# Group 1's values by seven products instead of eight, with M's sums on VectorE and new orders on ScalarE, VectorE and TensorE

## The chip, the cores and the metric

The kernel runs on one core of a Trainium2 chip. The metric is the device time of one execution in microseconds; several executions give a median. The profile is of one execution.

## The reference, cut to what matters

The input is 64 graphs of 128 nodes with 512 features each, an adjacency of 128x128 for each graph, and three 512x512 matrices.

```
h = maximum(layernorm(x), 0.0)
output = einsum('bni,io->bno', h, weight)            # the values
alpha = einsum('bno,bmo->bnm', h @ wq, h @ wk)
alpha = maximum(alpha, 0.0) * (adj != 0)
alpha = softmax(alpha, axis=1)
x = x + einsum('bnm,bmo->bno', alpha, output)
```

## The kernel before, in words

**Groups.** The 64 graphs are worked in 16 groups of 4, groups 0 to 15. The kernel first folds wq and wk into one matrix M, so that the scores are h M h'. Each group then has two large products, h with M (called t in the names) and h with the weight (called v), then the scores (s_bank, 48 matmuls of 128 columns), the softmax, and the output, the product of probabilities and values (12 matmuls of 512 columns). Every operand is split into a float16 high half and a float16 low half, and every product is three matmuls: high by high, high by low, low by high.

**Eight and seven products.** The plain form of a large product (`whole_product_v`, `whole_product_t`) is 48 matmuls of 512 columns. From group 2 on (`FIRST = 2`) both are made by a Strassen-like scheme (`product_v`, `product_t`): seven products P1 to P7 of 12 matmuls each, of 256 columns, into the PSUM banks TA, TB, TE (t) and VA, VB, VE (v). It needs four sums of quadrants of h (S1 to S4, `sums_of_h`, made on GpSimd, split by `hi_of_sum` on ScalarE and `lows_of_sums` on GpSimd, and transposed by DMA), four sums of the weight (wt) and of M (mt), a copy of P1 and of P5 by ScalarE (`copy_p1_t`, `copy_p5_t` and the same for v), and two additions on VectorE (`sum_x`, `sum_c22`). Groups 0 and 1 use the plain form.

**Order.** All orders are written out by hand, one in-order queue for each engine, with semaphores between them. Before group g's period, its h must be ready: VectorE takes the statistics (`stats`, L831, and the aggregate L834), GpSimd makes scale and shift (`layernorm_scales`, five small operations, L405 to L412), ScalarE normalises (`normalise_h`, L537, four graphs) and makes the high halves (`hi_of_h`, L547), GpSimd makes the low halves (L417) and S1 (L425), S3 (L428), S2 (L432), S4 (L436), where S1 waits for all four normalised graphs. SyncE's queue then issues the DMA transposes.

Two places in ScalarE's order matter. The high halves of S1 and S3 of group 3 (L552) stand ahead of `copy_p1_t` of group 2 (L574), and those of S2 and S4 of group 3 ahead of `hi_of_p` of group 1 (L656), the high halves of the probabilities. TensorE's P2 of t in group 2 waits for `copy_p1_t`, since P2 adds into the bank that the copy reads. TensorE's output products of group 1 (`outs`, L1175 to L1177) wait for the low halves of the probabilities (L908, VectorE), which wait for L656.

Of the kernel before, what the change touches and what calls it, by code (L numbers as in the profile page):

```python
# [5 lines left out]
def graph_attention_kernel(nc, x, adj, weight, wq, wk, out):  # L6
# [24 lines left out]
    FIRST = 2  # L31
    LOOPED = FIRST + 1
# [30 lines left out]
    def made_v(g, n):  # L63

        if isinstance(g, int) and g == LAST and n in (N_P2, N_P6):
            n = N_P2 + N_P6 - n
        return made(g, n)
# [4 lines left out]

    def sums(g, n):

        return 4 * g + (n - 4 * FIRST)

# [9 lines left out]
    with ctx:  # L86
# [44 lines left out]
        mt32 = spare  # L131
# [42 lines left out]
        M_BANK = [bank[k][:] for k in range(K)]  # L174

        def v_bank(g):

            return M_BANK if g == 1 else [bank[VB][:], bank[VE][:], bank[FREE][:], bank[TA][:]]


        def out_bank(g):

            if isinstance(g, int) and g == 0:
                return [bank[VB][:], bank[VE][:], bank[FREE][:], s_flat]
# [85 lines left out]
        def sum_turn(i, j):  # L270

            return i * (UNROLL // 2) + j // 2

# [3 lines left out]
        def _(sp):  # L277
# [98 lines left out]
        def _(pool):  # L376
# [106 lines left out]
            nc.gpsimd.tensor_tensor(mt32[:, T3], m32[:, HK:, HD:], m32[:, 0:HK, HD:], ALU.subtract).then_inc(mt_summed, 1)  # L483
            pool.wait_ge(mt_summed, 1)
            nc.gpsimd.tensor_tensor(mt32[:, T2], m32[:, HK:, HD:], mt32[:, T1], ALU.subtract).then_inc(mt_summed, 1)
            layernorm_scales(2)
            pool.wait_ge(mt_summed, 3)
            nc.gpsimd.tensor_tensor(mt32[:, T4], m32[:, HK:, :HD], mt32[:, T2], ALU.subtract).then_inc(mt_summed, 1)
            lo_of_h(2, 0, 0)
            lo_of_h(2, 0, 1)  # L490
            sum_s1(2)
            sum_s3(2)
            lo_of_h(2, 0, 2)
            lo_of_h(2, 0, 3)
            sum_s2(2)
            sum_s4(2)
# [24 lines left out]
            o = x_sb[:, LAST % UNROLL, 0]  # L521
# [3 lines left out]
        def _(act):  # L525
# [14 lines left out]
            def hi_of_h(g, s, b, turns=0, sum_turns=0):  # L540
# [4 lines left out]
                if b == 0 and not (isinstance(sum_turns, int) and sum_turns == 0):  # L545
                    act.wait_ge(sT_landed[s], 2 * 16 * sum_turns)
# [20 lines left out]
            def copy_p1_t(g):  # L567
# [45 lines left out]
            def hi_of_v22(g):  # L613
                act.wait_ge(v_summed, done(g, 2))
# [20 lines left out]
            def hi_of_whole_v(g, b):  # L635
# [4 lines left out]
                nc.scalar.activation(v_hi[:, b], v_bank(g)[b], ACT.Copy, scale=T_SCALE).then_inc(v_hi_made, 1)  # L640
# [780 lines left out]
```

## Time and profile before

| | us |
|---|---|
| median of 3 runs | 414.24 (414.03 to 414.66) |
| profiled execution, its own time | 414.27 |
| its span in the trace | 412.4 |
| busy: PE / DVE / ACT / POOL | 405.8 / 298.1 / 277.8 / 264.5 |

PE is TensorE, DVE is VectorE, ACT is ScalarE, POOL is GpSimd. The time outside the span is 1.9 us. TensorE's granted clock is 1.00 in every slice, which is the 2.4 GHz level. A busy time close to the span means that the engine is hardly ever without work; for the others, the idle time is spent waiting, and costs something only where TensorE waits for them.

### The profile page before, as it was taken

How to read it: one execution, taken by the hardware profiler on the slowest of the kernel's cores; microseconds unless marked ns; L12 is line 12 of the kernel's file. 1: busy time of each engine (PE TensorE's matmuls, PEld its weight loads, DVE VectorE, ACT ScalarE, POOL GpSimd, SP SyncE). 2: the span in 40 equal slices, each digit the busy share in tenths (PEclk: the TensorE clock that was granted, in tenths of full speed). 3: DMA queues.
4: the chain of work that ended last, by engine and by line, in shares of the span. 5: the costliest groups of instructions: out<-in, count | busy, mean ns of one | idle time of the engine just before them, and what ended most of it. 6: DMA issues, size and time to landing. Idle time of an engine off the chain costs nothing.

```text
span 412.4 us, 9484 instructions
## 1 busy us (share of the span) xinstructions
PE 405.8 (98%) x3581; PEld 321.9 (78%) x3581; DVE 298.1 (72%) x569; ACT 277.8 (67%) x590; POOL 264.5 (64%) x284
## 2 busy tenths in 40 slices
PE   8999999999999999999999999999999999999995
PEld 5444545979798897979798797979889797979883
DVE  5797789895867776776767777676777667556565
ACT  4749887766867677766777776776867776643534
POOL 0767896979495876859495775939577584910003
PEclk9999999999999999999999999999999999999999
DMA  8973858998969897896979497896988599393022
GB/s 299 367 98 69 215 105 224 225 206 209 218 170 191 237 155 210 193 206 183 188 219 192 131 240 200 200 214 174 188 252 157 154 219 234 41 187 100 2 103 102
DMA packets 161641, 75.03 MB, mean 182 GB/s; under 512 B 135360, under 2 KB 143808, under 8 KB 161600
## 3 DMA queue, kind: packets, MB, share of 16 engines
q1 hardware_dynamic: 161024, 73.55, 77.4%
q10 hardware_dynamic: 576, 0.92, 0.6%
q8 instruction: 28, 0.46, 0.5%
q14 instruction: 13, 0.11, 0.1%
HBM read 24.12 MB, written 16.78 MB: 99 GB/s over the span
## 4 chain that ended last, share of the span: by engine, by line
PE 82%; DVE 7%; ACT 4%; POOL 3%; issue 2%; DMA 2%; SPq 1%; DVEq 0%; ACTq 0%; POOLq 0%
PE bank L1139 10%; PE bank L1142 10%; PE bank L1141 10%; PE bank L1154 9%; PE bank L1157 9%; PE bank L1156 9%; PE s_bank L1170 3%; PE s_bank L1169 3%; PE s_bank L1168 3%; PE bank L1175 2%; PE bank L1177 2%; PE bank L1176 2%; DMA x_sb<-in_x 2%; POOL hn_lo L417 1%; ACT h L537 1%
## 5 line engine op out<-in xcount | busy, mean ns | idle before, releaser
L417 POOL TENSOR_TENSOR hn_lo<-h,hn_hi 128x512 f16<-128x512 f32 x64 | 74.5, 1174 | 54.0 <-ACT hn_hi L547 53.7
L537 ACT ACTIVATE h<-x_sb,shift,rstd 128x512 f32<-128x512 f32 x64 | 49.9, 804 | 23.6 <-POOL shift L412 23.3
L443 POOL TENSOR_TENSOR hn_lo<-s,hn_hi 128x512 f16<-128x512 f32 x56 | 63.3, 1161 | 0.3 <-ACT hn_hi L552 0.3
L1156 PE MATMUL bank<-wt_lo,hT_hi 128*128 128x256 f16 x224 | 61.1, 273 | 0.0
L1141 PE MATMUL bank<-hT_lo,mt_hi 128*128 128x256 f16 x224 | 61.1, 273 | 0.0
L1154 PE MATMUL bank<-wt_hi,hT_hi 128*128 128x256 f16 x224 | 61.1, 273 | 0.0
L1142 PE MATMUL bank<-hT_hi,mt_lo 128*128 128x256 f16 x224 | 61.1, 273 | 0.0
L1139 PE MATMUL bank<-hT_hi,mt_hi 128*128 128x256 f16 x224 | 61.1, 273 | 0.0
L1157 PE MATMUL bank<-wt_hi,hT_lo 128*128 128x256 f16 x224 | 61.1, 273 | 0.0
L552 ACT ACTIVATE hn_hi<-s 128x512 f16<-128x512 f32 x56 | 33.7, 625 | 24.1 <-POOL s L432 19.7
L1157 PE MATMUL bank<-w_hi,hT_lo 128*128 128x256 f16 x168 | 45.8, 273 | 0.0
L1156 PE MATMUL bank<-w_lo,hT_hi 128*128 128x256 f16 x168 | 45.8, 273 | 0.0
L1139 PE MATMUL bank<-hT_hi,m_hi 128*128 128x256 f16 x168 | 45.8, 273 | 0.0
L1142 PE MATMUL bank<-hT_hi,m_lo 128*128 128x256 f16 x168 | 45.8, 273 | 0.0
L1141 PE MATMUL bank<-hT_lo,m_hi 128*128 128x256 f16 x168 | 45.8, 273 | 0.0
L1154 PE MATMUL bank<-w_hi,hT_hi 128*128 128x256 f16 x168 | 45.8, 273 | 0.0
L845 DVE SCALAR_TENSOR_TENSOR tT_lo<-bank,tT_hi 128x512 f16<-128x512 f32 x42 | 28.9, 689 | 22.7 <-ACT tT_hi L605 17.2
L850 DVE SCALAR_TENSOR_TENSOR v_lo<-bank,v_hi 128x512 f16<-128x512 f32 x42 | 28.7, 684 | 21.6 <-ACT v_hi L623 21.6
L1168 PE MATMUL s_bank<-tT_hi,hT_hi 128*128 128x128 f16 x256 | 43.7, 219 | 0.0
L1169 PE MATMUL s_bank<-tT_lo,hT_hi 128*128 128x128 f16 x256 | 43.7, 219 | 0.0
L1170 PE MATMUL s_bank<-tT_hi,hT_lo 128*128 128x128 f16 x256 | 43.7, 219 | 0.0
L547 ACT ACTIVATE hn_hi<-h 128x512 f16<-128x512 f32 x64 | 39.2, 618 | 0.1
(166 smaller groups left out, 1105.0 us busy)
## 6 DMA issues: line engine op xcount, KB each, us to landing
out_h<-x_sb SPq DMA_DIRECT2D x62, 256.0 KB, 2.1
x_sb<-in_x SPq DMA_DIRECT2D x15, 1024.0 KB, 5.5
adj_sb<-in_adj SPq DMA_DIRECT2D x16, 256.0 KB, 5.3
hn_hi<-in_L_gnn_wq SPq DMA_DIRECT2D x4, 256.0 KB, 5.6
x_sb<-in_x SPq DMA_DIRECT2D x2, 512.0 KB, 7.2
w_sb<-in_L_gnn_weight SPq DMA_DIRECT2D x2, 512.0 KB, 8.6
hn_lo<-in_L_gnn_wk SPq DMA_DIRECT2D x2, 256.0 KB, 3.6
hn_lo<-in_L_gnn_wk ACTq DMA_DIRECT2D x2, 256.0 KB, 3.8
```

Of the source, the lines that this page charges most:

```text
L417: nc.gpsimd.tensor_tensor(hn_lo[:, s, b], h[:, b], hn_hi[:, s, b], ALU.subtract).then_inc(h_split, 1)
L443: nc.gpsimd.tensor_tensor(low, s32[:, f], high, ALU.subtract).then_inc(s_split, 1)
L537: nc.scalar.activation(h[:, b], x_sb[:, s, b], ACT.Relu, bias=shift[:, b:b + 1], scale=rstd[:, b:b + 1]).then_inc(h_made, 1)
L1139: nc.tensor.matmul(o, bh[:, k, cols], ah[:, :, k], start=first and c == 0 and k == 0, stop=False, skip_group_check=True)
L1141: nc.tensor.matmul(o, bh[:, k, cols], al[:, :, k], start=False, stop=False, skip_group_check=True)
L1142: last = nc.tensor.matmul(o, bl[:, k, cols], ah[:, :, k], start=False, stop=k == HK - 1, skip_group_check=True)
L1154: nc.tensor.matmul(o, ah[:, r, k], bh[:, k], start=first and r == 0 and k == 0, stop=False, skip_group_check=True)
L1156: nc.tensor.matmul(o, ah[:, r, k], bl[:, k], start=False, stop=False, skip_group_check=True)
L1157: last = nc.tensor.matmul(o, al[:, r, k], bh[:, k], start=False, stop=k == HK - 1, skip_group_check=True)
L1168: nc.tensor.matmul(o, hT_hi[:, s, b, k], tT_hi[:, k, b], start=k == 0, stop=False)
L1169: nc.tensor.matmul(o, hT_hi[:, s, b, k], tT_lo[:, k, b], start=False, stop=False)
L1170: last = nc.tensor.matmul(o, hT_lo[:, s, b, k], tT_hi[:, k, b], start=False, stop=k == K - 1)
```

## The change

Part 1: group 1's v is made by the seven products (84 matmuls of 256 columns for 48 of 512). So S1 to S4 of group 1 are made, split and transposed as well, and its P1 and P5 copied. Part 2: the four sums of M (into `mt32`) move from GpSimd to VectorE. Part 3: orders. TensorE's whole t products of group 1 use other banks, so that three of them come ahead of the wait for the last values of group 0; ScalarE and VectorE have another order in group 1. Part 4: in the last group, the quadrant C12 of v is split ahead of C22, the outputs of graphs 0 and 1 wait for two splits and not three, and graph 1 in place of graph 0 is finished by ScalarE and GpSimd. DMA waits for hT and sT use one count.

```diff
 (GpSimd)
             layernorm_scales(1)
-            for b in range(GB):
-                lo_of_h(1, 1, b)
-
-            pool.wait_ge(m_copied, K)
-            nc.gpsimd.tensor_tensor(mt32[:, T1], m32[:, 0:HK, HD:], m32[:, 0:HK, :HD], ALU.subtract).then_inc(mt_summed, 1)
...
+            sums_of_h(1, 1)
             layernorm_scales(2)
...
+            lows_of_sums(1, 1)
+            pool.wait_ge(s_split, sums(2, 0))
+            sums_of_h(2, 0)
 (ScalarE)
             hi_of_whole_t(0, 2)
+            hi_of_sum(1, 1, 0, S1)
+            hi_of_sum(1, 1, 1, S3)
...
             hi_of_whole_t(0, 3)
+            hi_of_sum(1, 1, 2, S2)
+            hi_of_sum(1, 1, 3, S4)
...
             hi_of_whole_t(1, 3)
+            copy_p1_v(1)
             hi_of_sum(2, 0, 2, S2)
             hi_of_sum(2, 0, 3, S4)
-            hi_of_whole_v(1, 0)
+            hi_of_v11(1)
+            copy_p5_v(1)
 (ScalarE, last group)
-            hi_of_p(LAST, range(HG))
+            hi_of_p(LAST, range(HG + 1))
+            hi_of_v12(LAST)
             hi_of_v22(LAST)
-            hi_of_v12(LAST)
-            hi_of_p(LAST, range(HG, GB))
+            hi_of_p(LAST, range(HG + 1, GB))
 (TensorE)
+            pe.wait_ge(hT_landed[1], 2 * 16)
+            for c in range(K - 1):
+                whole_product_t(1, c)
             pe.wait_ge(v_split, GB)
-            pe.wait_ge(hT_landed[1], 2 * 16)
-            for c in range(K):
-                whole_product_t(1, c)
+            whole_product_t(1, K - 1)
+            product_v(1, N_P1, bank[VA][:], True)
             pe.wait_ge(p_split, GB)
...
+            pe.wait_ge(v_copied, done_v(1, 1))
+            product_v(1, N_P2, bank[VA][:], False)
...
+            pe.wait_ge(out_read, HG)
+            product_v(1, N_P5, bank[VE][:], True)
...
+            product_v(1, N_P6, bank[VB][:], False)
+            scores(1, 1, quadrants=False)
...
+            pe.wait_ge(v_summed, done_v(1, 1))
...
+            product_v(1, N_P7, bank[VB][:], False)
+            product_v(1, N_P3, bank[VE][:], False)
...
+            pe.wait_ge(v_summed, done_v(1, 2))
...
+            product_v(1, N_P4, bank[VB][:], False)
...
-                pe.wait_ge(v_split, GB * LAST + (3 if b < HG else 4))
+                pe.wait_ge(v_split, GB * LAST + (2 if b < HG else 4))
```

VectorE before, in group 1 (L960 is a low half of t, L831 and L834 the statistics of group 3, L913 an output of group 0 added to x, L878 a mask, L983 a low half of M's sums):

```order
L960 SCALAR_TENSOR_TENSOR tT_lo<-bank2,tT_hi 128x512
L831 BN_STATS raw_stats<-x_sb 128x6
L834 BN_AGGR mean_var<-raw_stats 128x2
L831 BN_STATS raw_stats<-x_sb 128x6
L834 BN_AGGR mean_var<-raw_stats 128x2
L960 SCALAR_TENSOR_TENSOR tT_lo<-bank3,tT_hi 128x512
L913 SCALAR_TENSOR_TENSOR x_sb<-bank4,out_unscale,x_sb 128x512
L913 SCALAR_TENSOR_TENSOR x_sb<-bank5,out_unscale,x_sb 128x512
L913 SCALAR_TENSOR_TENSOR x_sb<-bank6,out_unscale,x_sb 128x512
L913 SCALAR_TENSOR_TENSOR x_sb<-s_bank,out_unscale,x_sb 128x512
L878 TENSOR_SCALAR mask<-adj_sb 128x512
L983 TENSOR_TENSOR mt_lo<-spare,mt_hi 128x512
```

VectorE in the change, the same stretch (L963 is the low half of t, L834 and L837 the statistics of group 3, L916 the outputs of group 0, L870 `sum_x_v` of group 1):

```order
L963 SCALAR_TENSOR_TENSOR tT_lo<-bank0,tT_hi 128x512
L834 BN_STATS raw_stats<-x_sb 128x6
L837 BN_AGGR mean_var<-raw_stats 128x2
L916 SCALAR_TENSOR_TENSOR x_sb<-s_bank,out_unscale,x_sb 128x512
L916 SCALAR_TENSOR_TENSOR x_sb<-bank5,out_unscale,x_sb 128x512
L834 BN_STATS raw_stats<-x_sb 128x6
L837 BN_AGGR mean_var<-raw_stats 128x2
L916 SCALAR_TENSOR_TENSOR x_sb<-bank1,out_unscale,x_sb 128x512
L916 SCALAR_TENSOR_TENSOR x_sb<-bank2,out_unscale,x_sb 128x512
L870 TENSOR_TENSOR bank5<-bank4,w_sb 128x512
L834 BN_STATS raw_stats<-x_sb 128x6
L837 BN_AGGR mean_var<-raw_stats 128x2
```

The last statistics of group 3 stood ahead of the outputs of group 0 and now stand behind them and behind `sum_x_v(1)`, which waits for P6 of group 1.

ScalarE before, from the first high half of h of group 3 to `copy_p1_t` of group 2 (L537 normalises, L547 is a high half of h, L640 one of a whole value, L552 those of S1 and S3 of group 3, L574 the copy):

```order
L547 ACTIVATE hn_hi<-h 128x512
L537 ACTIVATE h<-x_sb,shift,rstd 128x512
L640 ACTIVATE v_hi<-bank1 128x512
L547 ACTIVATE hn_hi<-h 128x512
L537 ACTIVATE h<-x_sb,shift,rstd 128x512
L640 ACTIVATE v_hi<-bank2 128x512
L547 ACTIVATE hn_hi<-h 128x512
L537 ACTIVATE h<-x_sb,shift,rstd 128x512
L547 ACTIVATE hn_hi<-h 128x512
L640 ACTIVATE v_hi<-bank3 128x512
L552 ACTIVATE hn_hi<-s32 128x512 x2
L574 ACTIVATE bank1<-bank0 128x512
```

ScalarE in the change, the same stretch behind the first normalised graph of group 3 (L535 normalises, L544 is a high half of h, L612, L616 and L620 those of C22, C12 and C21 of v, L549 those of S1 and S3 of group 3, L571 the copy):

```order
L612 ACTIVATE v_hi<-w_sb 128x2x256
L544 ACTIVATE hn_hi<-h 128x512
L535 ACTIVATE h<-x_sb,shift,rstd 128x512
L616 ACTIVATE v_hi<-bank5 128x2x256
L544 ACTIVATE hn_hi<-h 128x512
L535 ACTIVATE h<-x_sb,shift,rstd 128x512
L620 ACTIVATE v_hi<-bank4 128x2x256
L544 ACTIVATE hn_hi<-h 128x512
L535 ACTIVATE h<-x_sb,shift,rstd 128x512
L544 ACTIVATE hn_hi<-h 128x512
L549 ACTIVATE hn_hi<-s32 128x512 x2
L571 ACTIVATE bank1<-bank0 128x512
```

Three high halves of v stand among the normalisations, each of which now waits for a product or a sum; one more stands ahead of the first high half of h. What follows, S1 and S3 and then the copy, is as before.

## Rows read from the trace of the kernel before

**Rows 1.** The page: span, and busy time of each engine.
```profile
span 412.4 us, 9484 instructions
...
PE 405.8 (98%) x3581; PEld 321.9 (78%) x3581; DVE 298.1 (72%) x569; ACT 277.8 (67%) x590; POOL 264.5 (64%) x284
```

**Rows 2.** Timeline of PE: start, length, line, operation, idle before it.
```profile
47.86 0.39 PE L1290 MATMUL bank<-hT_hi,m_hi 128*128 128x512 f16 x1 [0.28 <-DVE v_lo L955]
...
60.82 0.38 PE L1281 MATMUL bank<-w_hi,hT_hi 128*128 128x512 f16 x1
...
71.18 0.22 PE L1168 MATMUL s_bank<-tT_hi,hT_hi 128*128 128x128 f16 x1
...
73.86 0.27 PE L1139 MATMUL bank<-hT_hi,m_hi 128*128 128x256 f16 x1
...
76.48 0.27 PE L1154 MATMUL bank<-w_hi,hT_hi 128*128 128x256 f16 x1
...
84.41 0.39 PE L1175 MATMUL bank<-v_hi,p_hi 128*128 128x512 f16 x1
...
86.87 0.39 PE L1175 MATMUL bank<-v_hi,p_hi 128*128 128x512 f16 x1 [0.34 <-DVE x_sb L913]
```

**Rows 3.** Timeline of ACT, group 3's h to the probabilities of group 1.
```profile
65.01 0.81 ACT L537 ACTIVATE h<-x_sb,shift,rstd 128x512 f32<-128x512 f32 x1 [0.81 <-POOL shift L412]
...
69.80 0.81 ACT L537 ACTIVATE h<-x_sb,shift,rstd 128x512 f32<-128x512 f32 x1
...
73.76 0.63 ACT L552 ACTIVATE hn_hi<-s 128x512 f16<-128x512 f32 x1 [0.60 <-POOL s L428]
75.37 0.58 ACT L574 ACTIVATE bank<-bank 128x512 f32<-128x512 f32 x1 [0.97 <-PE bank L1142]
...
80.38 0.62 ACT L552 ACTIVATE hn_hi<-s 128x512 f16<-128x512 f32 x1
80.90 1.27 ACT L656 ACTIVATE p_hi<-exps,row_inv 128x128 f16<-128x128 f32 x4
```

**Rows 4.** Timeline of POOL: scales, sums and low halves of group 3.
```profile
62.98 0.20 POOL L405 TENSOR_TENSOR var_eps<-mean_var,eps 128x4 f32<-128x4 f32 x1 [0.44 <-DVE mean_var L834]
...
64.78 0.20 POOL L412 TENSOR_TENSOR shift<-neg_mean,rstd 128x4 f32<-128x4 f32 x1
...
70.68 1.82 POOL L425 TENSOR_TENSOR s<-h 128x512 f32<-128x512 f32 x1 [1.06 <-ACT h L537]
72.47 1.26 POOL L428 TENSOR_TENSOR s<-h 128x512 f32<-128x512 f32 x1
73.69 2.72 POOL L417 TENSOR_TENSOR hn_lo<-h,hn_hi 128x512 f16<-128x512 f32 x2
76.37 1.26 POOL L432 TENSOR_TENSOR s<-s,h 128x512 f32<-128x512 f32 x1
77.72 1.27 POOL L436 TENSOR_TENSOR s<-h,s 128x512 f32<-128x512 f32 x1
```

**Rows 5.** Timeline of DVE: low halves (v, probabilities, M's sums) and statistics.
```profile
47.11 0.69 DVE L955 SCALAR_TENSOR_TENSOR v_lo<-bank,v_hi 128x512 f16<-128x512 f32 x1 [2.72 <-ACT v_hi L640]
...
53.56 4.35 DVE L908 SCALAR_TENSOR_TENSOR p_lo<-exps,row_inv,p_hi 128x128 f16<-128x128 f32 x4 [0.47 <-ACT p_hi L656]
...
62.02 0.66 DVE L831 BATCH_NORM_STATS2 raw_stats<-x_sb 128x6 f32<-128x512 f32 x1
62.72 0.18 DVE L834 BATCH_NORM_AGGREGATE mean_var<-raw_stats 128x2 f32<-128x6 f32 x1
...
66.36 0.69 DVE L983 TENSOR_TENSOR mt_lo<-spare,mt_hi 128x512 f16<-128x512 f32 x1
...
72.62 1.67 DVE L983 TENSOR_TENSOR mt_lo<-spare,mt_hi 128x512 f16<-128x512 f32 x1
...
81.71 2.65 DVE L908 SCALAR_TENSOR_TENSOR p_lo<-exps,row_inv,p_hi 128x128 f16<-128x128 f32 x4
```

**Rows 6.** Timeline of PE: first output product of the last group.
```profile
405.51 0.38 PE L1175 MATMUL bank<-v_hi,p_hi 128*128 128x512 f16 x1 [0.35 <-DVE v_lo L850]
```

More of the change, by code:

```diff
@@ L31, in graph_attention_kernel @@
     FIRST = 2
+    FIRST_V = 1
     LOOPED = FIRST + 1
@@ L63, in made_v, with done_v @@
     def made_v(g, n):
+        if isinstance(g, int) and g == FIRST_V and n in (N_P2, N_P5):
+            n = N_P2 + N_P5 - n
         if isinstance(g, int) and g == LAST and n in (N_P2, N_P6):
             n = N_P2 + N_P6 - n
-        return made(g, n)
+        return 7 * g + (n - 7 * FIRST_V)
     def done(g, n):
         return 2 * g + (n - 2 * FIRST)
+    def done_v(g, n):
+        return 2 * g + (n - 2 * FIRST_V)
     def sums(g, n):
-        return 4 * g + (n - 4 * FIRST)
+        return 4 * g + (n - 4 * FIRST_V)
     def whole(g, n):
@@ L174, in graph_attention_kernel, with t_bank @@
         M_BANK = [bank[k][:] for k in range(K)]
[L176 to L178 removed]
+        V0_BANK = [bank[VB][:], bank[VE][:], bank[FREE][:], bank[TA][:]]
+        def t_bank(g):
+            return [bank[k][:] for k in (TB, TE, FREE, TA)] if g == 1 else M_BANK
         def out_bank(g):
             if isinstance(g, int) and g == 0:
[L184 removed]
+                return [s_flat, bank[VE][:], bank[TB][:], bank[TE][:]]
             if isinstance(g, int) and g == LAST:
@@ L359, in _ @@
             load_adj(3)
+            sp.wait_ge(s_hi_made, sums(1, 4))
+            transpose_part(hT_hi, hn_hi, 1, GB, sT_landed)
             sp.wait_ge(mt_summed, 4)
             load_x(3)
+            sp.wait_ge(s_split, sums(1, 4))
+            transpose_part(hT_lo, hn_lo, 1, GB, sT_landed)
             for g in range(1, G):
                 period(g)
-            for b in (1, 2):
-                sp.wait_ge(out_read, GB * LAST + b)
+            for n, b in enumerate((0, 2)):
+                sp.wait_ge(out_read, GB * LAST + n + 1)
                 sp.dma_start(out_dram[:, GB * LAST + b:GB * LAST + b + 1, :],
@@ L544, in hi_of_h @@
                     act.wait_ge(hT_landed[s], 2 * 16 * turns)
-                if b == 0 and not (isinstance(sum_turns, int) and sum_turns == 0):
-                    act.wait_ge(sT_landed[s], 2 * 16 * sum_turns)
+                    act.wait_ge(sT_landed[s], 2 * 16 * turns)
                 nc.scalar.activation(hn_hi[:, s, b], h[:, b], ACT.Copy).then_inc(h_hi_made, 1)
@@ L1060, in _ @@
             lo_of_whole_t(1, 1)
+            lo_of_whole_t(1, 2)
             stats_all(3, 3, 0)
+            lo_of_whole_t(1, 3)
             stats_all(3, 3, 1)
-            lo_of_whole_t(1, 2)
+            residual(0, 0, 0)
+            residual(0, 0, 1)
             stats_all(3, 3, 2)
+            residual(0, 0, 2)
+            residual(0, 0, 3)
+            sum_x_v(1)
             stats_all(3, 3, 3)
-            lo_of_whole_t(1, 3)
-            for b in range(GB):
-                residual(0, 0, b)
-            make_mask(2, 0, 2)
-            lo_of_mt(0)
-            lo_of_whole_v(1, 0)
-            lo_of_mt(1)
-            lo_of_whole_v(1, 1)
-            lo_of_wt(3)
-            lo_of_whole_v(1, 2)
-            lo_of_mt(2)
-            lo_of_whole_v(1, 3)
+            lo_of_wt(3)
+            lo_of_v(1, 0, bank[VA][:], 0, 0)
+            sum_c22_v(1)
+            lo_of_mt(0)
+            lo_of_v(1, 1, c22_v, 1, 1)
+            lo_of_v(1, 2, bank[VE][:], 0, 1)
+            lo_of_v(1, 3, bank[VB][:], 1, 0)
+            lo_of_mt(1)
+            lo_of_mt(2)
+            make_mask(2, 0, 2)
             lo_of_mt(3)
@@ L1102, in _ @@
             lo_of_v(LAST, 0, bank[VA][:], 0, 0)
-            lo_of_v(LAST, 1, c22_v, 1, 1)
-            lo_of_v(LAST, 2, bank[VE][:], 0, 1)
+            lo_of_v(LAST, 1, bank[VE][:], 0, 1)
+            lo_of_v(LAST, 2, c22_v, 1, 1)
             lo_of_v(LAST, 3, bank[VB][:], 1, 0)
-            for b in range(1, GB - 1):
+            for b in (0, 2):
                 residual(LAST, LAST % UNROLL, b)
```

133 lines of the change are left out of this document (61 added, 72 removed).

## The prediction

> **What bounds the kernel now.** I read the page first: TensorE is busy 405.8 of 412.4 us [rows 1], so the kernel is as long as TensorE's work plus its few gaps, and the start and the tail. Then the timeline of TensorE, for its gaps. Behind the first matrices there are three of any size that the change touches: 0.28 us ahead of the t products of group 1, for the last low half of group 0's values; 0.34 us inside the output products of group 1; and 0.35 us ahead of the outputs of the last group [rows 2, 6]. Last the timelines of ScalarE, GpSimd and VectorE between 60 and 85 us, because the change reorders them there, and a change that saves TensorE's work is worth something only if they deliver earlier too. The reader should see that the softmax of group 1 was just in time: `p_lo` starts at 81.71 and lasts 2.65, and the output products start at 84.41 [rows 5, 2].
>
> **What the seven products save.** The 48 matmuls of group 1's values take 60.82 to 71.18, 10.36 us, or 0.216 each [rows 2]. A seven-product block is 12 matmuls; two of them take 73.86 to 76.48, so 1.31 each and 9.17 for seven. Saved: 1.19 us. The reordered t products can hide the 0.28 wait, since only the fourth needs that bank. Together 1.47 us, if TensorE is fed.
>
> **What they add.** GpSimd: four sums and four low halves of group 1, at 1.26 to 1.82 and about 1.2 us [rows 4], less the four sums of M that leave it. Two of those sums come ahead of the last low halves of h, so group 2's scales come about 1 us later. I cost that at nothing: the t products of group 1 (10.36 us) cover it; without cover it would be that 1 us. ScalarE: four high halves of sums and two copies, some 0.5 to 0.6 each; it was idle in this stretch (0.81 ahead of 65.01, [rows 3]). SyncE's queue: two more transposes, landing well ahead of P5, at no cost. VectorE: the sums of M, three of them ahead of the softmax of group 0, where it waited 2.72 us [rows 5]. The nearest row, a low half of M's sums, takes 0.69 to 1.67 us [rows 5]. Three at 0.69 are 2.1 us and fit; at 1.67 they are 5.0, and group 0's probabilities come up to 2 us late, of which the product P1 and the fourth t product hide about 1. I take nothing, and keep 0 to 1.
>
> The Trainium skill ("GPSIMD Engine Reference", section Key points) says that GpSimd shares its SBUF interfaces with VectorE, with contention for instructions of two SBUF inputs, and that VectorE is about twice as fast for elementwise work. The trace agrees in kind: the same four small operations on the probabilities last 4.35 us in one place and 2.65 in another [rows 5]. By that rule the sums of M are a gain without contention, and a cost only while GpSimd runs.
>
> **Where the new wait is.** This is the step that decides. The last statistics of group 3 end at 62.90 before [rows 5]. In the change they stand behind `sum_x_v(1)`, which waits for P6 of group 1. TensorE: t products start at 47.6 (47.86 less the wait), end at 47.6 + 10.36 = 57.95; P1 to 59.3; four outputs (12 matmuls of 0.216, 2.6) to 61.9; P2 to 63.2. P5 waits for the second output of group 0 to be read by VectorE, which stands behind low halves and two statistics; I make it 63.7 (0 to 1 us late). P6 ends at 66.3. The addition takes 0.2 to start and 0.6, the statistics with their aggregate 0.88 (62.02 to 62.90): 68.0. GpSimd's scales take 2.0 (62.98 to 64.98 [rows 4]): 70.05, against 64.98 before. So group 3's h starts 5.1 us later.
>
> From there the queues are what they were, and longer. ScalarE normalises four graphs: 65.01 to 70.61 before, 5.6 us [rows 3]; now one high half of v more (0.5) and a wait of 0.2 for `sum_c22_v(1)`, 6.3: 76.4. GpSimd's S1, S3, two low halves, S2, S4 take 70.61 to 78.99, 8.4 us [rows 4]: S1 and S3 at 79.5, S4 at 84.8.
>
> Who waits: (1) `copy_p1_t` of group 2 stands behind the high half of S3 in ScalarE's queue. Before, it waited 0.97 for TensorE [rows 3]; now it starts at 80.1, ends 80.65. TensorE, done with the scores of group 1 and P4 at about 73.0 (0.9 ahead of 73.86), wants to start P2 of t at 78.2: a gap of 2.4. (2) The high halves of the probabilities stand behind that of S4: 84.8 + 0.6 = 85.4, against 80.90. From that start to the end of `p_lo` it was 3.46 us before, 0.4 of it other work of VectorE: now 3.0, and the output products start at 88.4. TensorE has its next four blocks (5.2 us) done by 85.9 at the earliest: a second gap of up to 2.5, in part ahead of P2 of v, which waits for the copy of v's P1 behind the exponentials on ScalarE. Net: 88.4 against 84.41, **4.0 us later**, with the 1.47 already in it. The 0.34 gap within the outputs stays as it is, since VectorE's additions stand between `p_lo` and the first output read, as before.
>
> Behind this, GpSimd is 1 to 1.5 us later against TensorE than before for group 4, and the low halves of group 2 are that much later. I add 0.2 (0 to 0.9). After it nothing of groups 3 to 14 changes.
>
> **The last group.** Two splits instead of three ahead of the first outputs, where TensorE waited 0.35 [rows 6]. C12 needs P3, done about 1.3 us ahead of P4, so its high and low halves end about when P4 does. I take 0.3 off (0 to 0.35); the stores at the end, one of them now issued last by ScalarE, may take some of it back.
>
> **Sum.** Against the profiled execution's 414.27 (span 412.4 and 1.9 around it; the median of the runs is 414.24): 4.0 + 0.2 - 0.3 = +3.9, so 418.2. Its own range: below, GpSimd's six operations at their shorter lengths (1.26 and 1.16, 7.3 instead of 8.4) and P5 not waiting (0.8 less in all, since then `sum_c22_v` is waited for): -1.9, 416.3. Above, `p_lo` at the 4.35 of the other row: +1.7, 419.9.
>
> **The rivals.**
> - *TensorE stays fed, faster.* One mechanism: group 3's h is ready in time for the copy. It decides at the scale of group 3: the output products start no later than 84.4 less the 1.5 saved if S4's high half ends by about 79.9, so if the scales are made by about 64.5 to 65. For it: GpSimd and ScalarE have idle time before, and ScalarE's copy waited 0.97. Against: the statistics cannot end before P6 does, and P6 cannot end before 65.7 even with no gap. Price: 1.19 + 0.28 + 0.3 off, 412.5. Chance 0.12.
> - *Late, but mostly caught up.* The high halves wait less than I sum up, and only the gap at the copy is left, about 1.1 against before at 80.65 less 79.10 (the 76.48 plus two blocks), with 0.3 off at the end: 415.0 to 416.3. For it: GpSimd's rows vary by 0.45. Against: S4 stands ahead of the probabilities on ScalarE. Chance 0.15, a fifth of it within the measurement.
> - *It spreads.* The statistics and sums of M on VectorE make group 0's probabilities late (up to 1), and group 3's scores wait too (0.9): 420 to 421.5. Chance 0.10.
> - My forecast: 0.63.
>
> A difference under 0.2% (0.8 us) can't be told from no change here. Faster 0.12, within 0.2% 0.03, slower 0.85. Range 415.0 to 420.0: the forecast's own, and the second case.
>
> **What the profile would show.** TensorE busy less by about 1.2 us. The wait at the t products of group 1 gone. The last statistics of group 3 ending near 68, the shift near 70, S1 starting near 76.5. `copy_p1_t` of group 2 no longer waiting for TensorE, but TensorE's P2 of t for it, near 80.7. The output products of group 1 near 88.4, preceded by a wait of about 2 us for `p_lo`. The gap of 0.35 in the last group gone or near it. I am wrong if the scales of group 3 are made before 67, or if TensorE shows no gap of over 1 us between 72 and 89.

## The result, and the profile after

The changed kernel takes 421.76 us (median of 6 runs, 421.29 to 422.6), the kernel before 414.31 (6 runs beside it): ratio 1.0185, 95% interval 1.0174 to 1.0195. It is slower, as forecast, but by 7.5 us where 3.9 were forecast, outside the range. The profiled execution took 421.77, its span 420.0 against 412.4.

The page of the kernel after, beside [rows 1]; of the slices, the row of TensorE:

```profile
span 420.0 us, 9597 instructions
...
PE 405.2 (96%) x3617; PEld 324.8 (77%) x3617; DVE 305.0 (73%) x575; ACT 280.5 (67%) x596; POOL 270.3 (64%) x288
...
PE   8999998769999999999999999999999999999995
```

TensorE has 0.6 us less busy time than before and 7.6 us more span. A slice is 10.5 us, so the three digits 8, 7, 6 lie between 63 and 94 us. The first row of products of group 2 starts 0.75 us later than before (74.61 for 73.86), group 1's outputs 7.69 later: nearly all of the loss lies between these two, in the first half of group 2's period. The timeline of TensorE after, every wait from the first scores on, beside [rows 2, 6]:

```profile
45.62 0.23 PE L1183 MATMUL s_bank<-tT_hi,hT_hi 128*128 128x128 f16 x1 [0.67 <-DVE tT_lo L963]
...
48.31 0.38 PE L1295 MATMUL bank<-hT_hi,m_hi 128*128 128x512 f16 x1
...
65.38 0.27 PE L1169 MATMUL bank<-wt_hi,hT_hi 128*128 128x256 f16 x1 [1.31 <-DVE x_sb L916]
...
77.77 0.28 PE L1169 MATMUL bank<-w_hi,hT_hi 128*128 128x256 f16 x1 [0.38 <-DVE v_lo L853]
...
82.65 0.28 PE L1154 MATMUL bank<-hT_hi,m_hi 128*128 128x256 f16 x1 [2.08 <-ACT bank L571]
...
87.22 0.28 PE L1169 MATMUL bank<-w_hi,hT_hi 128*128 128x256 f16 x1 [1.78 <-ACT bank L580]
...
92.10 0.39 PE L1190 MATMUL bank<-v_hi,p_hi 128*128 128x512 f16 x1 [2.09 <-DVE p_lo L911]
...
94.56 0.39 PE L1190 MATMUL bank<-v_hi,p_hi 128*128 128x512 f16 x1 [0.34 <-DVE x_sb L916]
...
413.04 0.38 PE L1190 MATMUL bank<-v_hi,p_hi 128*128 128x512 f16 x1 [0.19 <-DVE v_lo L853]
```

Read the starts against [rows 2, 6]: group 1's outputs 7.69 later (92.10 for 84.41), the fourth of them 7.69 too (94.56 for 86.87), the last group's outputs 7.53 (413.04 for 405.51). Nothing is lost or regained from the fourth output up to the last group.

Why TensorE waits stands on the other engines. VectorE, its timeline after (beside [rows 5]):

```profile
69.53 0.18 DVE L837 BATCH_NORM_AGGREGATE mean_var<-raw_stats 128x2 f32<-128x6 f32 x1
...
77.02 0.69 DVE L853 SCALAR_TENSOR_TENSOR v_lo<-bank,v_hi 128x512 f16<-128x512 f32 x1 [1.01 <-ACT v_hi L620]
77.63 1.28 DVE L986 TENSOR_TENSOR mt_lo<-mt,mt_hi 128x512 f16<-128x512 f32 x2
78.83 1.50 DVE L881 TENSOR_SCALAR mask<-adj_sb 128x512 bf16<-128x512 int32 x1
80.25 1.75 DVE L986 TENSOR_TENSOR mt_lo<-mt,mt_hi 128x512 f16<-128x512 f32 x1
81.92 0.68 DVE L889 SCALAR_TENSOR_TENSOR alpha<-s_bank,maskT 128x512 f32<-128x512 f32 x1
...
89.41 2.63 DVE L911 SCALAR_TENSOR_TENSOR p_lo<-exps,row_inv,p_hi 128x128 f16<-128x128 f32 x4
```

ScalarE and GpSimd after, the rows that answer to [rows 3, 4]:

```profile
72.25 0.81 ACT L535 ACTIVATE h<-x_sb,shift,rstd 128x512 f32<-128x512 f32 x1 [4.76 <-POOL shift L423]
...
81.48 0.63 ACT L549 ACTIVATE hn_hi<-s 128x512 f16<-128x512 f32 x1 [0.77 <-POOL s L439]
82.01 0.58 ACT L571 ACTIVATE bank<-bank 128x512 f32<-128x512 f32 x1
84.18 0.49 ACT L629 ACTIVATE exps<-alpha,shift_max,s_unscale 128x128 f32<-128x128 f32 x1 [1.59 <-DVE shift_max L894]
...
88.09 0.62 ACT L549 ACTIVATE hn_hi<-s 128x512 f16<-128x512 f32 x1
88.61 1.27 ACT L653 ACTIVATE p_hi<-exps,row_inv 128x128 f16<-128x128 f32 x4
```

```profile
78.29 1.75 POOL L436 TENSOR_TENSOR s<-h 128x512 f32<-128x512 f32 x1 [1.25 <-ACT h L535]
...
85.43 1.26 POOL L447 TENSOR_TENSOR s<-h,s 128x512 f32<-128x512 f32 x1
```

The last statistics of group 3 end at 69.7 (62.9 before), group 3's first normalisation starts at 72.25 (65.01), the copy at 82.01 (75.37), and S4 is made at 86.7. That is the forecast chain. The row that it did not have is that of the exponentials: at 84.18 they still waited 1.59 us for VectorE, whose softmax of group 1 (`alpha`, 81.92) stood behind three low halves of M's sums and a mask. Before, only one low half stood ahead of `alpha`, which started at 74.20; the rest was done earlier, between the outputs of group 0 and the low halves of v.

### The profile page after: what moved, and what is told of

Its sections match the earlier page's. It is cut to its first block, busy times and chain, and to the rows that moved or that the text cites. A ratio compares the mean times of both kernels' runs of the same rounds, so it can differ in the third digit from the quotient of the medians.

```text
span 420.0 us, 9597 instructions
## 1 busy us (share of the span) xinstructions
PE 405.2 (96%) x3617; PEld 324.8 (77%) x3617; DVE 305.0 (73%) x575; ACT 280.5 (67%) x596; POOL 270.3 (64%) x288
## 4 chain that ended last, share of the span: by engine, by line
PE 77%; DVE 9%; ACT 5%; POOL 4%; issue 2%; DMA 2%; SPq 1%; DVEq 0%; ACTq 0%; POOLq 0%
PE bank L1169 10%; PE bank L1172 10%; PE bank L1171 10%; PE bank L1156 10%; PE bank L1154 10%; PE bank L1157 10%; PE s_bank L1184 3%; PE s_bank L1183 3%; PE s_bank L1185 3%; PE bank L1190 2%; PE bank L1192 2%; PE bank L1191 2%; ACT h L535 2%; DMA x_sb<-in_x 2%; DVE p_lo L911 2%
## 5 line engine op out<-in xcount | busy, mean ns | idle before, releaser
L454 POOL TENSOR_TENSOR hn_lo<-s,hn_hi 128x512 f16<-128x512 f32 x60 | 68.8, 1179 | 0.0
L535 ACT ACTIVATE h<-x_sb,shift,rstd 128x512 f32<-128x512 f32 x64 | 50.0, 803 | 27.8 <-POOL shift L423 27.3
L1169 PE MATMUL bank<-wt_hi,hT_hi 128*128 128x256 f16 x240 | 65.4, 273 | 1.3 <-DVE x_sb L916 1.3
L1172 PE MATMUL bank<-wt_hi,hT_lo 128*128 128x256 f16 x240 | 65.4, 273 | 0.0
L1171 PE MATMUL bank<-wt_lo,hT_hi 128*128 128x256 f16 x240 | 65.4, 273 | 0.0
L549 ACT ACTIVATE hn_hi<-s 128x512 f16<-128x512 f32 x60 | 36.1, 627 | 26.3 <-POOL s L443 20.4
L1169 PE MATMUL bank<-w_hi,hT_hi 128*128 128x256 f16 x180 | 49.1, 273 | 2.2 <-ACT bank L580 1.8
L1172 PE MATMUL bank<-w_hi,hT_lo 128*128 128x256 f16 x180 | 49.1, 273 | 0.0
L1171 PE MATMUL bank<-w_lo,hT_hi 128*128 128x256 f16 x180 | 49.1, 273 | 0.0
L853 DVE SCALAR_TENSOR_TENSOR v_lo<-bank,v_hi 128x512 f16<-128x512 f32 x45 | 30.8, 684 | 23.7 <-ACT v_hi L620 22.1
L629 ACT ACTIVATE exps<-alpha,shift_max,s_unscale 128x128 f32<-128x128 f32 x64 | 30.8, 482 | 14.1 <-DVE shift_max L894 14.1
```

The lines of the kernel that those rows point to most:

```text
L454: nc.gpsimd.tensor_tensor(low, s32[:, f], high, ALU.subtract).then_inc(s_split, 1)
L535: nc.scalar.activation(h[:, b], x_sb[:, s, b], ACT.Relu, bias=shift[:, b:b + 1], scale=rstd[:, b:b + 1]).then_inc(h_made, 1)
L1169: nc.tensor.matmul(o, ah[:, r, k], bh[:, k], start=first and r == 0 and k == 0, stop=False, skip_group_check=True)
L1171: nc.tensor.matmul(o, ah[:, r, k], bl[:, k], start=False, stop=False, skip_group_check=True)
L1172: last = nc.tensor.matmul(o, al[:, r, k], bh[:, k], start=False, stop=k == HK - 1, skip_group_check=True)
```

## The experiments

Theory L (late): group 3's statistics behind `sum_x_v(1)` make its scales, its h and its sums late, and ScalarE's copy and probabilities of the next stage stand behind them. Theory E: the exponentials' wait for VectorE's leftovers is an equal second half. Rival W: the work that seven products add in group 1 (sums, low halves, copies) is what costs, in whatever order. They were tested by other orders of the changed kernel and by parts put into the kernel before; times are medians, each against the kernel before on the same chip.

**1. Lateness without the change** (`e5_late`), the kernel before:

```diff
-            stats_all(3, 3, 3)            (ahead of lo_of_whole_t(1, 3))
             lo_of_mt(1)
+            stats_all(3, 3, 3)
             lo_of_whole_v(1, 1)
```

> The kernel before, with only the last statistics of group 3 put late, behind two low halves of M's sums, as late as the change has them (end near 69 instead of 62.9). Nothing of the change is in it. Theory A with C: the scales come near 71.1, group 3's h 6.1 us late, the probabilities of group 1 at about 87 instead of 80.9, and the kernel 5 to 6 us slower: 419.3 to 420.3. Rival B (the added work is the cause): under 1 us slower, below 415.3.

Measured: 419.49, ratio 1.0133 (1.0116 to 1.015), inside what was expected. Moving two small instructions by 5.4 us (their end is at 68.33 for 62.90) costs 5.4 us. Its TensorE waits at places of the changed kernel, and so do VectorE and ScalarE:

```profile
84.72 0.28 PE L1154 MATMUL bank<-w_hi,hT_hi 128*128 128x256 f16 x1 [1.35 <-ACT bank L583]
...
89.62 0.39 PE L1175 MATMUL bank<-v_hi,p_hi 128*128 128x512 f16 x1 [2.10 <-DVE p_lo L908]
```

```profile
73.13 0.69 DVE L955 SCALAR_TENSOR_TENSOR v_lo<-bank,v_hi 128x512 f16<-128x512 f32 x1 [4.80 <-ACT v_hi L640]
...
81.69 0.49 ACT L632 ACTIVATE exps<-alpha,shift_max,s_unscale 128x128 f32<-128x128 f32 x1 [1.59 <-DVE shift_max L891]
```

The outputs are 5.2 us later than in [rows 2]. So lateness costs this without W: none of the change's work is in this kernel. It does not separate L from E. The late h held up the high halves of v on ScalarE, VectorE waited 4.80 us for one of them, and then its leftovers stood ahead of the softmax here too: S4 was made at 84.2, the high halves of the probabilities started at 86.12, 1.3 us after S4's high half could have ended.

**2. Statistics early, in the change** (`e1_stats`):

```diff
+            stats_all(3, 3, 3)
             residual(0, 0, 2)
             residual(0, 0, 3)
             sum_x_v(1)
-            stats_all(3, 3, 3)
```

> The change, with one VectorE step moved: the last statistics of group 3 ahead of the outputs of graphs 2 and 3 of group 0 and of sum_x_v(1), instead of behind them. Theory A (the late statistics delay group 3's h, and h delays everything behind it): the scales of group 3 are made near 69.3 instead of 72.2; P4 of group 1 (done at 74.6) now limits the high half of C21, which stands ahead of the last normalised graph, so that the h chain gains about 1.5 us: about 420.3 in all. Rival B (it is the added work of part 1 that costs, wherever it stands): no gain, 421.8. Rival C (the softmax of group 1, held by VectorE's leftover low halves of M and the mask, is the bound): no gain unless C21's low half comes earlier too.

Measured: 421.94, ratio 1.0195 (1.0171 to 1.0219): no gain, where Theory A expected 420.3. ScalarE after this edit:

```profile
68.81 0.82 ACT L535 ACTIVATE h<-x_sb,shift,rstd 128x512 f32<-128x512 f32 x1 [1.49 <-POOL shift L423]
72.75 0.63 ACT L612 ACTIVATE v_hi<-w_sb 128x512 f16<-128x512 f32 x1 [3.13 <-DVE w_sb L874]
```

The scales came 3.4 us earlier and bought nothing: the high half of C22, which stands ahead of the first high half of h, waits 3.13 us for a sum that needs P7. The statistics were one of two late gates at nearly the same time, 0.2 us apart (the high half of C22 starts at 72.75 here and at 72.97 in the change). The prediction had this second wait, of 0.2 us, but only as a small addition to the first.

**3. VectorE's leftovers early** (`e2_mt`), and **both** (`e3_both`):

```diff
             lo_of_v(1, 0, bank[VA][:], 0, 0)
+            lo_of_mt(0)
+            lo_of_mt(1)
             sum_c22_v(1)
-            lo_of_mt(0)
+            make_mask(2, 0, 2)
             lo_of_v(1, 1, c22_v, 1, 1)
+            lo_of_mt(2)
             lo_of_v(1, 2, bank[VE][:], 0, 1)
+            lo_of_mt(3)
             lo_of_v(1, 3, bank[VB][:], 1, 0)
-            lo_of_mt(1)
-            lo_of_mt(2)
-            make_mask(2, 0, 2)
-            lo_of_mt(3)
```

> The change, with VectorE's low halves of M's sums and the mask of group 2 moved forward, into its idle time between the low halves of group 1's v, instead of behind them. Statistics stay late. Theory C (the probabilities of group 1 were held by VectorE, whose softmax_shift(1) stood behind 1.28, 1.50 and 1.75 us of such work, and ScalarE's exponentials waited 1.59 us for it): softmax_shift(1) starts near 78.5 instead of 81.9, the exponentials follow the copy at once, and the probabilities are then bound by S4 of group 3 (ready at 86.7 where they started at 88.6): 1.4 us gained, about 420.4. Theory A alone (only group 3's sums hold the probabilities): nothing gained, 421.8.

> The change with both moves: the last statistics of group 3 early, and VectorE's low halves of M's sums and the mask in its idle time. If A and C are both links of the chain, the gains add to about 2.9 us: 418.9. If only one of them binds, no more than the better of the two alone. Rival B: 421.8.

Measured: 421.36 (1.0173, 1.0156 to 1.019) and 421.21 (1.0162, 1.0145 to 1.0179), where 420.4 and 418.9 were expected; by these intervals neither can be told from the change. In `e3_both` the exponentials started at 81.58, 2.6 us earlier than in the change, and p_hi at 86.00 instead of 88.61: E's mechanism is real. But little of it arrived, and in `e2_mt`, which lacks the early statistics, nearly the same is seen (wait of 3.11 us ahead of the outputs). The VectorE of `e3_both`, its TensorE at the outputs, and its windows (busy time of TensorE, weight loads, VectorE, ScalarE, GpSimd; granted clock; DMA):

```profile
86.91 3.52 DVE L911 SCALAR_TENSOR_TENSOR p_lo<-exps,row_inv,p_hi 128x128 f16<-128x128 f32 x4
```

```profile
90.50 0.61 PE L1190 MATMUL bank<-v_hi,p_hi 128*128 128x512 f16 x1 [3.10 <-DVE p_lo L911]
90.90 0.63 PE L1191 MATMUL bank<-v_lo,p_hi 128*128 128x512 f16 x1
91.32 0.63 PE L1192 MATMUL bank<-v_hi,p_lo 128*128 128x512 f16 x1
```

```profile
85.00:90.00 5.00, 2.40 (x22) 1.90 (x20) 4.97 (x9) 2.76 (x8) 5.00 (x6) 1.00 0.88 166
90.00:95.00 5.00, 4.50 (x16) 1.90 (x17) 4.44 (x9) 2.81 (x5) 2.61 (x7) 0.66 0.72 163
```

Two things took it back. The low halves of the probabilities now ran beside GpSimd's low halves and took 3.52 us, not 2.63. And where the change has three waits of about 2 us, this kernel has 0.83, 0.96 and 3.10, and behind the last the granted clock fell to its 1.2 GHz level: the first output matmuls start some 0.42 us apart, not 0.22, and 1.6 us are lost.

**4. ScalarE's order too** (`e6_act`, `e7_three`, `e8_fed`). `e6_act` is `e1_stats` with the three late high halves of v behind group 3's h; `e7_three` has `e2_mt`'s edit as well; `e8_fed` has the moves for TensorE's earlier waits in addition (outputs of group 0 read ahead of low halves of t, and t's last high half ahead of two of the weight's sums), and a slightly other order of VectorE's leftovers.

```diff
             normalise_h(3, 3, 0)
-            hi_of_v22(1)
             hi_of_h(3, 1, 0, turn(0, 1))
             normalise_h(3, 3, 1)
-            hi_of_v12(1)
             hi_of_h(3, 1, 1)
             normalise_h(3, 3, 2)
-            hi_of_v21(1)
...
             hi_of_h(3, 1, 3)
+            hi_of_v22(1)
+            hi_of_v12(1)
+            hi_of_v21(1)
```

> The change, with the last statistics of group 3 early (as in the first run, which gained nothing), and on ScalarE the high halves of C22, C12 and C21 of group 1's v moved behind the eight operations on group 3's h, instead of among them. Theory D (after the first run: the high half of C22, which waits for P7 of group 1 and stood ahead of the first high half of group 3's h, held the chain 3.1 us just as the statistics had; both must go): h of group 3 is normalised by 73.2 instead of 78.2, the copy in group 2 comes in time, and the softmax of group 1, still behind VectorE's 4.5 us of leftovers, sets the rest: its probabilities at 87 instead of 88.6, 1.6 us gained, about 420.2, less if TensorE's clock falls. If the queue order on ScalarE does not matter: 421.9 as in the first run.

> The same, and VectorE's leftovers (low halves of M's sums, mask) in its idle time. Theory D with C: the softmax of group 1 is found near 77.5 and the exponentials run near 80; the high half of S4 (81.7) no longer holds anything; the probabilities start near 84.3 instead of 88.6, and the outputs of group 1 at 87.5 instead of 92.1: about 417.2. Rival B (the added work itself costs): no better than 421.

> The same, and three more moves for TensorE's two earlier gaps: graphs 0 and 1 of group 0 are added to x ahead of the other work of VectorE (P5's wait, 1.31 us), sum_x_v(1) ahead of graphs 2 and 3, and the low halves of t of group 0 ahead of the second low half of the weight's sums, with ScalarE's high half ahead of the weight's (the scores' wait, 0.67). If the gaps before group 2 add to the end, 1.5 to 2 us better than the run before it, 415.2 to 415.7, near the kernel before. If they are covered by later waits (the probabilities again), no better than the run before it.

Measured: 422.08 (1.0197, 1.0182 to 1.0213), 417.87 (1.0091, 1.0076 to 1.0106), 419.15 (1.0122, 1.0106 to 1.0137). With L's two gates open but VectorE's leftovers in place (`e6_act`), nothing is gained, since the exponentials wait 7.34 us for them, and the clock falls behind a wait of 5.80 us. With all three (`e7_three`), half of the loss is gone, close to what was expected. So L and E are two locks on one door, each hiding the other. What is left in `e7_three` stands at one place. The three high halves of v, now behind h on ScalarE, make their low halves late; TensorE waits for the last of them ahead of group 2's first v product, and the clock falls behind that wait:

```profile
79.44 0.28 PE L1169 MATMUL bank<-w_hi,hT_hi 128*128 128x256 f16 x1 [2.28 <-DVE v_lo L853]
```

```profile
80.00:85.00 5.00, 5.00 (x33) 3.86 (x31) 3.98 (x9) 3.92 (x13) 4.83 (x5) 0.66 1.23 214
```

From the end of the product ahead of it to the start of this one it is 2.45 us, and the six blocks behind it take 9.53 us where six at 1.31 are 7.86, so some 1.7 went to the clock.

`e8_fed` missed what it hoped for (415.2 to 415.7). It brought TensorE to that place 2.0 us earlier and the low half that it waits for only 0.3 us earlier, so that the wait grew:

```profile
79.17 0.28 PE L1169 MATMUL bank<-w_hi,hT_hi 128*128 128x256 f16 x1 [4.03 <-DVE v_lo L853]
```

```profile
80.00:85.00 5.00, 5.00 (x33) 3.85 (x32) 4.00 (x9) 2.41 (x10) 4.68 (x4) 0.66 1.24 169
```

The clock cost the same in both kernels: here too the six blocks took 9.53 us. That `e8_fed` is 1.3 us slower than `e7_three` comes from VectorE: one more low half of M's sums stood ahead of `alpha`, the high halves of the probabilities started at 87.02 for 85.51, and TensorE waited 0.78 us for `p_lo` and 0.34 inside the outputs, where `e7_three` has no wait.

**5. Softmax first, leftovers last** (`e10_early`, `e13_tail`, `e14_order`), three tries at an order in which seven products pay.

```diff
+            softmax_shift(1, 1, 1)              (e10: ahead of all low halves of v)
             lo_of_v(1, 0, bank[VA][:], 0, 0)
...
             softmax_sum(g - 1)                  (e13: group 2's period)
+            lo_of_p(g - 1)
+            mean_variance(g + 2, b), lo_of_mt(2)
...
+            lo_of_sum(3, 1, 1, S3)              (e14: GpSimd)
+            layernorm_scales(4)
+            lo_of_sum(3, 1, 2, S2)
```

> The change, with every link found so far taken off: the moves of the run with three more moves, and (a) softmax_shift(1) on VectorE ahead of the low halves of group 1's v, of M's sums and of the mask, (b) on ScalarE, in group 2, the copy of P1, the exponentials and the copies of P5 and of v's P1 ahead of the high halves of S1 and S3 of group 3, and the probabilities ahead of those of S2 and S4, (c) C22, C12 and C21 of v between the operations on h, each no earlier than it is ready. If the chain found is the whole cause (late statistics, C22 ahead of h, VectorE's leftovers ahead of the softmax), TensorE has no wait over 0.5 us before group 2's outputs, these start near 83 (84.4 in the kernel before), and the kernel gets the saving of the seven products: 412.4 to 413.2. If the added work of part 1 itself costs (rival B), it stays above 414.2.

> The whole change, with the orders of the last try (group 1's softmax early on VectorE, copies ahead of the sums on ScalarE) and, new, VectorE's leftovers behind the low halves of the probabilities of group 1: two low halves of M's sums, the mask of group 3 and the aggregates of group 4. All four high halves of group 3's sums stand behind the probabilities on ScalarE. Theory: what remained of the loss was VectorE's queue alone. Then row_inv is made at about 78.3, p_hi starts near 79 to 79.5, p_lo near 80, the output products start when TensorE has done its four blocks, near 83.7, and the time is 413 to 414.2, at or below the kernel before. Rival: GpSimd's sums and low halves of group 3, which run at the same time, stretch p_lo to 3.5 us or more, and the work put off makes the additions and splits of group 2 late: outputs after 85, or new waits of TensorE between 85 and 95, and 415 to 417.

> The last try with three more moves around group 1's outputs. VectorE: the sum of the exponentials ahead of the statistics of group 4 (which waited 3.47 us for the load of their x, with row_inv behind them), one low half of M's sums into the idle time ahead of it, the first low half of t right behind the probabilities, the first output of group 0's successor read ahead of the two additions. ScalarE: t's first high half ahead of those of the sums. GpSimd: group 4's scales between the low halves of group 3's sums instead of behind them. Theory, that only the orders of the queues stand between the seven products and their gain: outputs near 83.7 as in the last try, the waits inside them (1.08, 1.19) down to 0.3 in all, those at the scores of group 2 (1.58 and 0.97) down to under 0.5, and the time 412.8 to 415. Rival, that the work of group 1's sums on GpSimd and VectorE does not fit here: the waits come back at another place of groups 2 and 3, four or more of them with 3 us or over in all, and the time is 416 to 419.

Measured: 419.99 (1.0139, 1.0123 to 1.0154), 419.59 (1.0135, 1.0115 to 1.0155), 418.17 (1.0093, 1.0076 to 1.011). All three miss what was hoped for (412.4 to 413.2, 413 to 414.2, 412.8 to 415). The case that the added work costs, in whatever order, came in `e10_early` (above 414.2) and in `e14_order` (416 to 419); `e13_tail` was slower than even that case had it (415 to 417). In `e10_early` the exponentials were on time (76.02), but VectorE was busy for 19.8 of the 20 us from 70 to 90, and one wait of 4.81 us ahead of the outputs lowered the clock again. In `e13_tail` the outputs came at 83.90, half a microsecond **earlier** than in [rows 2], and still the kernel is 5.4 us slower. Its five longest waits behind that, of which only the second had one before it in [rows 2] (0.34 us):

```profile
86.29 0.39 PE L1204 MATMUL bank<-v_hi,p_hi 128*128 128x512 f16 x1 [0.92 <-DVE tT_lo L846]
...
88.14 0.39 PE L1204 MATMUL bank<-v_hi,p_hi 128*128 128x512 f16 x1 [1.03 <-DVE x_sb L914]
...
98.54 0.22 PE L1197 MATMUL s_bank<-tT_hi,hT_hi 128*128 128x128 f16 x1 [1.42 <-DVE tT_lo L846]
...
100.85 0.23 PE L1197 MATMUL s_bank<-tT_hi,hT_hi 128*128 128x128 f16 x1 [0.81 <-DVE tT_lo L846]
...
110.94 0.28 PE L1183 MATMUL bank<-w_hi,hT_hi 128*128 128x256 f16 x1 [0.72 <-ACT bank L580]
```

`e14_order`, 3.9 us slower than the kernel before, is rid of two of these five waits (0.92 and 1.42). The other three are still there (1.92 inside the outputs, 0.81 at the scores of group 2, 0.70 at group 3's P2 of v), with three more of 0.3 to 0.6. Its low halves of the probabilities, and those of `e13_tail`, which had GpSimd idle for one microsecond beside them:

```profile
79.98 4.34 DVE L914 SCALAR_TENSOR_TENSOR p_lo<-exps,row_inv,p_hi 128x128 f16<-128x128 f32 x4 [0.47 <-ACT p_hi L658]
```

```profile
82.72 1.12 DVE L909 SCALAR_TENSOR_TENSOR p_lo<-exps,row_inv,p_hi 128x128 f16<-128x128 f32 x4
```

So W is right in a second line: the order explains about half of the loss, and the rest, in part at new places and in part at the old ones, did not vanish in the orders tried. That no order at all can do it is not shown. Nor was the other split of the change run: the seven products in the order of the kernel before, or the new orders (part 3) without the seven products.

**6. The other parts alone**, in the kernel before: the last group (`e9_last`), M's sums on VectorE (`e11_msums`), and both (`e12_parts`).

```diff
-            hi_of_p(LAST, range(HG))            (e9: ScalarE, with the rest of part 4)
+            hi_of_p(LAST, range(HG + 1))
+            hi_of_v12(LAST)
...
-            nc.gpsimd.tensor_tensor(mt32[:, T1], ...)   (e11: four sums)
+            nc.vector.tensor_tensor(mt32[:, T1], ...)
```

> The kernel before, with only part 4 of the change: in the last group C12 split ahead of C22, outputs of graphs 0 and 1 waiting for two splits, and graph 1 finished by ScalarE and GpSimd. My forecast for this part was 0.3 us off; the trace of the change shows TensorE's wait 0.19 instead of 0.35. Expected now: 0.1 to 0.2 us off, 0.02 to 0.05%, too little for certain; the gap in the trace near 0.19. A rival, that the stores at the end take it back: no change of the span.

> The kernel before, with only part 2 of the change: M's four sums on VectorE instead of GpSimd, three ahead of the low half of the last values of group 0, the fourth behind softmax_shift(0). I took nothing for this part, with 0 to 1 us of loss. VectorE was idle for 2.7 us there, and three sums at the 0.60 us from start to start of the change's trace fit. GpSimd makes group 2's scales about 4 us earlier, so the last values of group 0 are split earlier and TensorE's wait of 0.28 ahead of group 1's t products goes: 0 to 0.3 us gained, 413.9 to 414.2. If VectorE and GpSimd hinder each other, up to 1 us lost.

> The kernel before with parts 2 and 4 of the change and nothing else: M's four sums on VectorE, and in the last group C12 split ahead of C22 with the first outputs waiting for two splits. Alone they gave 413.41 against 414.14 and 413.89 against 414.23. If they are independent, and they sit 350 us apart, their gains add: 0.73 + 0.34 = 1.1 us, so about 413.1. Rival: either gain is mostly the spread of the medians, and the two together give 413.5 or more.

Measured: 413.89 against 414.23 (0.9990, 0.9981 to 0.9999), 413.41 against 414.14 (0.9988, 0.9979 to 0.9997), 413.63 against 414.21 (0.9989, 0.998 to 0.9998). Each is a small gain, by an interval that only just leaves out a ratio of 1; the first two are larger than the 0.1 to 0.2 us and the 0 to 0.3 us that were expected. By the medians the two together gain no more than either, 0.6 us where 1.1 was expected, and the rival (413.5 or more) seems right. The traces say otherwise. The first t product of group 0 starts at 31.77 in the kernel before and at 31.58, 31.34 and 32.33 in these three, though their edits come behind it; from it to the first output of the last group it is 373.74, 373.60, 373.14 and 373.00 us. So the gains inside are 0.14, 0.60 and 0.74, and they add; the start, which differs by up to 1 us from profile to profile, hides it. The wait of the last group falls from 0.35 to 0.19 [rows 6] in `e9_last`, the one ahead of group 1's t products (0.28, [rows 2]) is gone in `e11_msums`. `e12_parts` has both:

```profile
86.85 0.39 PE L1175 MATMUL bank<-v_hi,p_hi 128*128 128x512 f16 x1 [0.30 <-DVE x_sb L906]
...
405.33 0.38 PE L1175 MATMUL bank<-v_hi,p_hi 128*128 128x512 f16 x1 [0.20 <-DVE v_lo L843]
```

All three are, by their medians, faster than the kernel before and than the change. `e12_parts` is the change without its seven products and without part 3's orders.

## Why the prediction's direction was right, and its size wrong

The forecast case came in: slower, through group 3's statistics behind `sum_x_v(1)`. Its signs appeared: TensorE's wait at the copy (2.08 in the row, 2.25 from block to block, for 2.4), a wait of 2.09 for `p_lo` at the outputs, the wait at group 1's t products gone, and that of the last group down from 0.35 to 0.19. TensorE's busy time fell by 0.6 and not by 1.2. I read this from the rows: a row of 256 columns is counted as 0.27 us long though the next starts 0.11 later, so that each wait adds some 0.16 of busy time; there are six new ones and one is gone, an estimated 0.8 in all. The time is 7.5 us longer and not 3.9; the outputs are off by 3.7 us (92.10 for 88.4), and the terms are these.

- **"the t products start at 47.6"**: 48.31, +0.7. The scores of group 0 waited 0.67 for a low half of t, behind two low halves of the weight's sums on VectorE that took 3.55 us (2.43 before). Nothing in the sum had this wait.
- **"P5 ... I make it 63.7 (0 to 1 us late)"**, so 0.5 taken: TensorE stood 1.48 there (1.31 in the row), +1.0. The first two outputs of group 0 were read behind four low halves and two statistics, and `p_lo` of group 0 had taken 5.01 us (4.35 in [rows 5]).
- **"GpSimd's scales take 2.0"**: 69.71 to 72.21, 2.5, +0.5. Up to here 2.2 us, of which 1.9 arrive at S4: 86.7 for 84.8, while GpSimd's six operations took the 8.4 us that were put down for them.
- **"The high halves of the probabilities stand behind that of S4"**: this is the step that failed. What held them was ScalarE's exponentials, which stand ahead of S4's high half in the queue and waited 1.59 us for VectorE; the sum had nothing for that. S4's high half could have ended at 87.3; p_hi started at 88.61. The sum went through ScalarE and GpSimd and never asked when VectorE could begin the softmax of group 1. Before, its leftovers were done at 74.3 [rows 5]; in the change they stood between the last low half of v (77.02) and `alpha` (81.92). That is +1.3, and "3.0" from p_hi to the outputs was 3.5 as before (VectorE's other work stayed between them), another +0.5. With the 1.9 at S4 this makes the 3.7.
- **"I add 0.2 (0 to 0.9)"** for what comes behind: 0. **"I take 0.3 off"** for the last group: 0.16.
- **Part 2, "I take nothing, and keep 0 to 1"**: alone it is a gain of 0.7 by the medians (`e11_msums`; 0.6 inside the trace), outside what was kept. In the change group 0's probabilities were late (`p_lo` at 54.93 for 53.56 before), but hardly through the sums of M: from the first score to `p_lo` it is 8.83 us before, 8.91 in `e11_msums` and 9.31 in the change. So the sums cost 0.1 there, the late scores 0.8 to 0.9, and 0.4 a normalisation and a high half of h that ScalarE's new order has ahead of the high halves of the probabilities.

The saving was sized right: the two blocks between 77.77 and 80.29 plus one matmul are 2.6 us, so seven are 9.2. The upper rival, *It spreads*, described the early waits; at 420 to 421.5 it still fell short. The upper bound of the range was made from `p_lo` alone, as if only one term could be long, when five terms of one chain (0.7, 1.0, 0.5, 1.3, 0.5) lay above their middle together. That the direction came out right is no luck, since `e5_late` shows the mechanism alone; that its wait of about 2 us for `p_lo` was met at 2.09 is luck, since both ends of that wait came later than forecast.

## What to carry to other kernels

When a step becomes late, follow it to every engine on which something of the next stage is queued behind it or behind work that used to fill idle time, and take the latest of them: here a second chain, 1.3 us longer, ended on VectorE, whose queue had been followed only up to the statistics. Moving one late gate shows nothing while a second stands 0.2 us behind it; such gates must be opened together before any is judged. And a saving of 1.2 us of TensorE's work in a start-up stage has to be paid for by four sums, eight splits, two copies and two additions on the other engines, of which VectorE, for one, was busy for 19.8 of 20 us in `e10_early`: in no order tried did it pay, while parts 2 and 4, which only move work, did by a little. A gain of 0.3 us is better read from distances inside a trace than from medians, when the start of a run differs by more.

## What the runs showed of the hardware

TensorE's granted clock fell behind single waits, and not behind as much waiting in pieces. In the change, waits of 2.08, 1.78 and 2.09 us with about 2.6 us of work between them left it at 1.00. Behind one wait of 3.10 us (`e3_both`) its mean was 0.66 in the next window of five microseconds, behind 4.03 (`e8_fed`) 0.66, behind 2.28 (`e7_three`) 0.66, behind 4.81 (`e10_early`) and 5.80 (`e6_act`) 0.59 to 0.73. Output matmuls of 512 columns then started 0.42 to 0.43 us apart instead of 0.216, which is the 1.2 GHz level for the 2.4 GHz level. That cost 1.6 us in `e3_both`, and 2.5 in `e10_early`, where all twelve output matmuls ran so: most of what the earlier softmax gained was lost to the clock. Why 2.28 us lowered it in one kernel and 2.09 us did not in another stays open.

VectorE's operations with two SBUF inputs lengthened while GpSimd ran: the same four operations on the probabilities lasted 1.12 us with GpSimd idle for most of it, and 2.63, 3.52, 4.34 and 5.01 beside it; a low half of M's sums 0.68 or 1.75. The mask, with one SBUF input, lengthened too (0.42 to 1.50). Others did not: one statistic took 0.69 us with GpSimd idle (`e5_late`), two took 1.26 beside a busy one (the change), and a low half of v, which reads a PSUM bank, took 0.68 beside a busy one (`e7_three`). The Trainium skill ("SBUF — State Buffer", section SBUF: two separate sides) says that the port pair which a VectorE instruction with two SBUF inputs shares with GpSimd is locked for a whole instruction and not shared by bandwidth. The trace agrees in kind, since 4.34 and 5.01 us are four times 1.1 and 1.25, about one GpSimd operation of 1.27 each; that the two engines take turns is argued from these lengths. By them, as an estimate, an operation of 128 columns costs there nearly what one of 512 does (1.03 to 1.75 for low halves of M's sums), and one in place of the four should help, if one instruction can do their work; that was not tried.
